# A six-layer transformer stage with its slots in a new order, an unrolled expert stage, and the softmax product on VectorE

## The reference, cut to what matters

```python
# mixture of experts: three routed linears, top 2 of 8 experts
logits = x @ router_w.T
vals, idx = top_k(logits, 2); probs = softmax(vals)
combine = einsum('tk,tke->te', probs, one_hot(idx, 8))
out = sum(combine[:, e:e+1] * (x @ expert_w[e].T) for e in range(8))

# transformer, 6 times: 16 heads of 64, windows of 32 tokens that see 64 keys
q, k, v = split(shift_tokens(x) @ Wqkv)
q = rotary(l2norm(q) * qs); k = rotary(l2norm(k) * ksc)
attn = softmax(8 * q k^T with mask)
x = (attn @ v) @ Wo + x
x = (a * gelu(gate)) @ W2 + b2 + x     # a, gate = split(norm(shift_tokens(x)) @ W1 + b1)
```

## Time and profile before

| | us |
|---|---|
| median of 3 runs | 5227.65 (5224.09 to 5231.3) |
| the profiled execution, its own time | 5220.35 |
| its span, first to last instruction | 5218.5 |
| PE busy | 4516.0 (87%) |
| DVE busy | 3483.4 (67%) |
| ACT busy | 2311.9 (44%) |
| POOL busy | 2147.3 (41%) |
| expert stage | about 110 to 1035 |
| transformer stage | about 1230 to 5218 |

### The profile page before, as it was taken

How to read it: one execution, slowest core, us unless ns; L and a number is a source line. 1 busy time by engine, 2 the same in 40 slices (tenths; PEclk the granted TensorE clock), 3 DMA queues, 4 the chain that set the end, 5 groups by cost and what they waited for, 6 DMA issues and landing times.

```text
span 5218.5 us, 147460 instructions
## 1 busy us (share of the span) xinstructions
PE 4516.0 (87%) x64229; PEld 3255.0 (62%) x64613; DVE 3483.4 (67%) x7580; ACT 2311.9 (44%) x4138; POOL 2147.3 (41%) x1332
## 2 busy tenths in 40 slices
PE   4999899885888888888888888888888888888887
PEld 3666666563666666666666666666666666666665
DVE  5434343435777777777777777777777777778884
ACT  2111111122555555555555555555555555555553
POOL 0000000003555555555555555555555555555552
PEclk7999999997999999999999989999999999999997
DMA  1000000001111111111111111111111111111110
GB/s 70 1 1 0 0 0 0 9 1 43 29 33 30 33 41 39 33 31 32 41 39 33 33 29 44 40 33 30 36 43 38 30 30 33 45 39 32 32 33 24
DMA packets 70585, 152.25 MB, mean 29 GB/s; under 512 B 14523, under 2 KB 43078, under 8 KB 69574
## 3 DMA queue, kind: packets, MB, share of 16 engines
q1 hardware_dynamic: 69958, 143.09, 9.4%
HBM read 27.69 MB, written 2.10 MB: 6 GB/s over the span
## 4 chain that ended last, share of the span: by engine, by line
PE 44%; DVE 22%; ACT 5%; issue 5%; POOL 0%; DMA 0%; SPq 0%; DVEq 0%; POOLq 0%; ACTq 0%
PE pQ L1480 8%; PE pS L1464 7%; PE pO L1524 6%; PE pC L1580 5%; PE pO L1511 4%; ACT sq L1355 4%; PE pM L1546 4%; PE pM L1535 3%; PE pT L1511 3%; DVE E L1196 3%; DVE mx L1194 2%; DVE rot L1216 2%; DVE m L1220 2%; DVE ve L1254 2%; DVE n L1231 2%
## 5 line engine op out<-in xcount | busy, mean ns | idle before, releaser
L1138 POOL TENSOR_TENSOR rot<-rot,m 128x1024 f32<-128x1024 f32 x384 | 905.1, 2357 | 602.8 <-DVE m L1220 602.8
L1130 POOL TENSOR_TENSOR rot<-rot,rn 128x1024 f32<-128x1024 f32 x384 | 731.9, 1906 | 281.1 <-DVE rn L102 281.1
L1147 POOL TENSOR_TENSOR E<-E,rc 128x512 f32<-128x512 f32 x384 | 400.5, 1043 | 943.1 <-DVE rc L1206 943.0
L1346 ACT ACTIVATE E<-E 128x512 f32<-128x512 f32 x384 | 241.7, 629 | 1091.5 <-DVE E L1196 1091.5
L1511 PE MATMUL pO<-PT,V 64*64 64x32 f32 x12288 | 482.5, 232 | 199.6 <-ACT PT L1362 199.6
L1194 DVE TENSOR_REDUCE mx<-pS 128x8 f32<-128x512 f32 x384 | 264.2, 688 | 548.6 <-PE pS L1464 548.4
L1511 PEld LDWEIGHTS pO<-PT,V 64*64 64x64 f32 x12288 | 440.9, 149 | 284.2 <-issue 284.2
L1464 PE MATMUL pS<-kT,qT 64*32 64x64 f32 x24576 | 493.1, 238 | 87.1 <-issue 57.3
L1464 PEld LDWEIGHTS pS<-kT,qT 64*32 64x32 f32 x24576 | 424.0, 120 | 172.2 <-issue 172.1
L1216 DVE TENSOR_TENSOR rot<-pQ,tabl 128x1024 f32<-128x1024 f32 x384 | 469.5, 1223 | 54.0 <-ACT sq L1355 52.0
L1511 PE MATMUL pT<-PT,V 64*64 64x32 f32 x12288 | 484.6, 233 | 0.0
(11 more groups left out here) (221 smaller groups left out, 7932.3 us busy)
## 6 DMA issues: line engine op xcount, KB each, us to landing
V<-V SPq DMA_DIRECT2D x192, 384.0 KB, 3.5
xs<-XT SPq DMA_DIRECT2D x192, 64.0 KB, 2.9
V<-V SPq DMA_DIRECT2D x96, 128.0 KB, 3.3
ys<-XT SPq DMA_DIRECT2D x192, 64.0 KB, 2.0
wq<-in_wqkv SPq DMA_DIRECT2D x6, 512.0 KB, 4.0
wk<-in_wqkv SPq DMA_DIRECT2D x6, 512.0 KB, 4.0
wv<-in_wqkv SPq DMA_DIRECT2D x6, 512.0 KB, 3.9
wo<-in_wo SPq DMA_DIRECT2D x6, 512.0 KB, 4.0
```

Of the source, the lines that this page charges most:

```text
L1130: e.tensor_tensor(r, r, rn[n % 2][:, u * HEADS:(u + 1) * HEADS].unsqueeze(2).to_broadcast([P, HEADS, HD]), ALU.mult)\
L1138: e.tensor_tensor(rot[j % RING][:, :], rot[j % RING][:, :], m2[:, :, :].rearrange("p h d -> p (h d)"), ALU.add)\
L1147: e.tensor_tensor(ev, ev, rc[:, g, :].unsqueeze(2).to_broadcast([P, NW, KEYS]), ALU.mult).then_inc(g_no.sem, 1)
```

## The change

Three things are changed.

1. In the expert stage the loop at run time is written out as straight code, and the staging copy b_xst goes, with its POOL slot and its semaphore. PE, DVE read X itself.
2. In the transformer stage the product E * rc goes from POOL (`by_sum`) to DVE, as the last instruction of `sums(B,g)` behind the reciprocal; `probs` on PE waits for DVE now.
3. The slot lists of all engines of the transformer stage are in another order. SP issues its transfers of V earlier in the pass, the weights wv at the end of the pass before, and the output later.

```diff
@@ moe_phase @@
-        xst = [sb(f"b_xst{i}", [P, L]) for i in range(2)]
...
-            run((0, 0), None)
-            run((1, 1), (0, 0))
-            with eng.Fori(0, (NSEQ - 2) // 2) as i:
-                for p in range(2):
-                    n = 2 * i + (2 + p)
-                    run((n, p), (n - 1, 1 - p))
-            run(None, (NSEQ - 1, 1))
+            for n in range(NSEQ + 1):
+                run((n, n % 2) if n < NSEQ else None, (n - 1, (n - 1) % 2) if n else None)
...
-                        e.wait_ge(gr.sem, gr.at("st", n))
...
-                            m = e.transpose(pm[0][:, t * P:(t + 1) * P], xst[p][:, t * P:(t + 1) * P], ident[:, :])
+                            m = e.transpose(pm[0][:, t * P:(t + 1) * P], X[:, n, t, :], ident[:, :])
@@ transformer_phase, gpsimd @@
-                unit_scale(R, 0)
-                root(C)
-                by_sum(B, 0)
-                rotary_add(A, 0)
-                last_root(F)
-                for k in range(1, 4):
+                for k in range(4):
                     unit_scale(R, k)
-                    by_sum(B, k)
                     rotary_add(A, k)
+                    if k == 0:
+                        root(C)
+                    if k == 1:
+                        last_root(F)
@@ vector, sums @@
                 e.reciprocal(rc[:, g, :], sm[:, g, :]).then_inc(v_r.sem, 1)
+                e.wait_ge(v_r.sem, v_r.at("rc", i))
+                ev = E[i % 2][:, :].rearrange("p (w k) -> p w k", k=KEYS)
+                e.tensor_tensor(ev, ev, rc[:, g, :].unsqueeze(2).to_broadcast([P, NW, KEYS]), ALU.mult).then_inc(v_r.sem, 1)
@@ vector, slots @@
-                statistics(C)
                 less_max(B, 0)
                 sums(B, 0)
+                rotate(A, 0)
+                statistics(C)
+                squares(A, 0)
                 normal(C)
...
@@ tensor, slots @@
                 scores(B, 0)
+                probs(Dn, 3)
                 project(A, 0)
-                probs(Dn, 3)
+                back(C)
+                attend(Dn, 3)
                 turn(R, 0)
...
@@ tensor, probs @@
-                e.wait_ge(g_no.sem, g_no.at("no", i))
+                e.wait_ge(v_r.sem, v_r.at("no", i))
```

More of the change, by code:

```diff
@@ L1084, in _ @@
                     e.dma_start(wqkv[1][:, :], I["wqkv"][A // NSEQ, :, N:2 * N]).then_inc(wqkv_l[1], 16)
-                if R and starts(R):
-                    e.wait_ge(p_v.sem, p_v.at("b", 2 * R - 1))
-                    e.dma_start(wqkv[2][:, :], I["wqkv"][R // NSEQ, :, 2 * N:3 * N]).then_inc(wqkv_l[2], 16)
                 if C and starts(C):
@@ L1102, in _ @@
                     e.dma_start(wqkv[0][:, :], I["wqkv"][(A + 1) // NSEQ, :, 0:N]).then_inc(wqkv_l[0], 16)
+                if F is not None:
+                    f = F - (NP - NSEQ)
+                    e.wait_ge(v_f.sem, v_f.at("out", f))
+                    e.dma_start(out[:, f, :, :], X[:, f, :, :]).then_inc(stored, 16)
                 if R is not None:
                     v, w = V[R % 2][:, :, 0, :], V[R % 2][:, :, 1, :]
-                    e.wait_ge(a_v.sem, a_v.at("b", 2 * R))
-                    e.dma_start(w[WIN:P, 0, :], v[0:P - WIN, 0, :]).then_inc(vs_l[R % 2], 16)
-                    e.dma_start(w[0:WIN, 1, :], v[P - WIN:P, 0, :]).then_inc(vs_l[R % 2], 16)
                     e.wait_ge(a_v.sem, a_v.at("b", 2 * R + 1))
                     e.dma_start(w[WIN:P, 1, :], v[0:P - WIN, 1, :]).then_inc(vs_l[R % 2], 16)
+                    if starts(R + 1) and R + 1 < NP:
+                        e.dma_start(wqkv[2][:, :], I["wqkv"][(R + 1) // NSEQ, :, 2 * N:3 * N]).then_inc(wqkv_l[2], 16)
             e.wait_ge(stored, 16 * NSEQ)
@@ L1305, in _ @@
                     tables(A)
-                statistics(C)
                 less_max(B, 0)
                 sums(B, 0)
+                rotate(A, 0)
+                statistics(C)
+                squares(A, 0)
                 normal(C)
-                rotate(A, 0)
-                squares(A, 0)
-                last_stats(F)
                 less_max(B, 1)
@@ L1317, in _ @@
                 squares(A, 1)
-                last_normal(F)
+                last_stats(F)
                 less_max(B, 2)
-                hidden(C, 0)
                 sums(B, 2)
@@ L1323, in _ @@
                 squares(A, 2)
+                last_normal(F)
                 less_max(B, 3)
+                hidden(C, 0)
+                sums(B, 3)
+                rotate(A, 3)
                 hidden(C, 1)
                 hidden(C, 2)
-                sums(B, 3)
-                rotate(A, 3)
-                ffn_add(C)
                 squares(A, 3)
                 roots(A)
+                ffn_add(C)
         @block.scalar
@@ L1403, in _ @@
             for A, R, B, Dn, C, F in passes():
+                probs(Dn, 3)
                 exponent(B, 0)
                 square(A, 0)
-                probs(Dn, 3)
+                heads_out(Dn, 3)
                 turned(R, 0)
-                heads_out(Dn, 3)
-                affine(C)
+                values(R, 0)
                 exponent(B, 1)
                 square(A, 1)
+                affine(C)
+                probs(B, 0)
+                turned(R, 1)
+                heads_out(B, 0)
+                probs(B, 1)
+                exponent(B, 2)
+                square(A, 2)
                 gelu(C, 0)
                 gelu(C, 1)
-                probs(B, 0)
-                turned(R, 1)
+                heads_out(B, 1)
+                turned(R, 2)
                 gelu(C, 2)
-                heads_out(B, 0)
-                exponent(B, 2)
-                square(A, 2)
-                probs(B, 1)
-                turned(R, 2)
-                heads_out(B, 1)
-                values(R, 0)
+                values(R, 1)
+                probs(B, 2)
                 exponent(B, 3)
                 square(A, 3)
-                probs(B, 2)
+                heads_out(B, 2)
                 turned(R, 3)
-                heads_out(B, 2)
-                values(R, 1)
         @block.tensor
@@ L1604, in _ @@
                 scores(B, 0)
+                probs(Dn, 3)
                 project(A, 0)
-                probs(Dn, 3)
+                back(C)
+                attend(Dn, 3)
                 turn(R, 0)
-                last(F)
-                attend(Dn, 3)
-                normed(C)
+                values(R, 0)
                 scores(B, 1)
                 project(A, 1)
+                normed(C)
+                combine(Dn)
+                probs(B, 0)
+                turn(R, 1)
                 hidden(C, 0)
-                probs(B, 0)
-                combine(Dn)
-                turn(R, 1)
+                attend(B, 0)
+                last(F)
+                scores(B, 2)
+                probs(B, 1)
+                project(A, 2)
+                attend(B, 1)
+                turn(R, 2)
                 hidden(C, 1)
-                attend(B, 0)
-                scores(B, 2)
-                project(A, 2)
+                values(R, 1)
+                scores(B, 3)
+                probs(B, 2)
+                project(A, 3)
                 hidden(C, 2)
-                probs(B, 1)
-                turn(R, 2)
-                attend(B, 1)
-                values(R, 0)
-                scores(B, 3)
-                project(A, 3)
-                contract(C)
-                probs(B, 2)
-                turn(R, 3)
-                attend(B, 2)
-                values(R, 1)
-                back(Dn)
+                attend(B, 2)
+                turn(R, 3)
+                contract(C)
 def layout(i):
```

37 lines of the change are left out of this document (10 added, 27 removed).

## The result

The changed kernel takes 5290.38 us (median of 3 runs, 5285.33 to 5291.64) against 5227.65. The ratio is 1.012, with a 95% interval of 1.0095 to 1.014: slower, 13 us under the forecast of 5303.

A forecast was written before the change was run, and what follows sets the result against it. No engine is full; a pass is a ring partly over DVE, partly over PE. 5220.35 + 155 (passes) + 5 (last layer) - 80 (expert stage) = 5300, left at 5303 us for the median; range 5195 to 5420.

The forecast's parts named there:

- The ring: Transformer pass as four segments between `less_max` on DVE and PE: 41.6 us at full clock, 3.1 over the undisturbed old order.
- Segment 3 and the product of group 1: PE from `normal(C)` to `less_max(B,2)`: 8.9 us, DVE waits 1.6 us, so the product there is hidden.
- The late Exp: Segment 1: copy `probs(B,2)` now precedes ACT's table load, so Exp starts at 2.39 instead of 1.45 us, +0.94.
- The clock: A fall to 1.2 GHz expected at the gap ahead of `contract`; half of 1.3 us taken, giving 42.2 us a pass.
- PE's new waits: PE waits about 2.5 us ahead of `contract`, 1.4 at `values(R,0)`, 1.1 at `normed`, 1.3 at `hidden(C,1)`.
- The total of the pass term: Transformer stage: +1.63 us a pass against 40.57, +155 us for 95 passes.
- The expert stage: PE's staging-copy wait goes, 53.4 us in 14 passes, plus 27 us of clock at 1.9 a pass: -80 us.
- The last layer and the ends: In the last layer F adds statistics and a norm where DVE now waits: +5 us at most.
- the removed wait decides: Rival: losing the wait at `attend(Dn,3)` makes passes 38.5 to 39.5 us, total 4990 us; chance 0.13.
- The two parts cancel: Rival: no clock falls, passes of 41.2 to 41.6 us, +60 to +98 against -80, about 5222 us; chance 0.17.
- Stalls against POOL: Rival: three products on DVE's path wait for POOL instructions, 3 us more a pass, 5590 us; chance 0.05.
- That straight code costs what the loop did: Rival: in the expert stage, fetching straight code costs as much, so that change brings nothing, 5380 us; chance 0.05.

The follow-up runs named there:

- second experiment: The whole change, but with the product (`by_sum`) back on POOL between `unit_scale` and `rotary_add`: 5119.87 us, ratio 0.979 to the kernel before.
- fifth experiment: The change, with `exponent(B,3)` and its table load ahead of the copy `probs(B,2)` on ACT: 5194.43 us, ratio 0.994 to the kernel before.
- the first: The change's expert stage alone, in front of the transformer stage of the kernel before: 5149.21 us, ratio 0.985.
- seventh experiment: The kernel before with only the expert stage's loop written out as straight code, staging copy kept: 5206.94 us, ratio 0.996.

## Why the prediction was right, point by point

The sign, the size and the mechanism came out: a pass that needs more DVE time than its removed wait was worth, less a gain in the expert stage. That the total is so near is in part luck: against the sum of the prediction the passes came out 20 us lower, the ends 10 lower and the expert stage 21 higher.

- **The ring.** Forecast at full clock 12.55 + 10.17 + 8.9 + 9.95 = 41.6; measured 12.62 + 10.17 + 9.13 + 9.83 = 41.75. Three segments are within 0.12 us. The 3.1 us more than the old order undisturbed are 3.26 at clock 1.00.
- **Segment 3 and the product of group 1.** This term was mis-sized. I held the product there for hidden behind PE; it costs 0.43 of segment 3's 9.13 us (second experiment). `attend(B,0)` waits for `attention_add` (L1221, 4064.40), which stands behind the product (4061.53) on DVE. The wait for it was counted, the product in front of it was not.
- **The late Exp.** Forecast +0.94 us, measured 1.0 when undone.
- **The clock.** I forecast 42.2 with a stretch at 1.2 GHz as long as before in half of the passes. The mean is 42.04. A short fall costs nothing, as forecast (41.75 at a mean clock of 0.96 and of 1.00). A long one costs 0.6 us instead of 1.3 and comes in 14 of the first 81 passes instead of half, but there are 5 passes of 44.0 that I had not foreseen. The two errors are of opposite sign.
- **The tables.** Missed. I looked for POOL beside the four products, found it idle, and was right there (the median of the product is 691 ns). I did not ask what else has two inputs in SBUF: `tables` now starts behind POOL's instruction, where it began ahead of it before, five times 2 us. The prediction had weighed this mechanism, but only for the four products.
- **PE's new waits.** `contract` 2.5 forecast, 2.67 in the pass shown; `hidden(C,1)` 1.3, measured 1.16; `values(R,0)` 1.4, measured 0.26; `normed` 1.1, measured 0.59. The means are 2.6, 1.2, 0.5 and 0.7. The last two lie behind a fall of the clock, which stretches PE's work and so shortens its wait. The fifth experiment fits this: 56 of its first 81 passes are at clock 1.00, and there the two waits have means of 1.1 and 1.0 us.
- **The total of the pass term.** +155 us for 95 passes; measured +134.9 for 92, which is 1.47 a pass instead of 1.63.
- **The expert stage.** -80 forecast. By itself it brings 82 us, but the changed kernel's own trace shows only 59 ahead of the first `less_max`. The wait went (53.4 us in all). The clock part failed there: I took 1.9 us a pass, and 0.8 is seen (14 passes are 65.0 us shorter, 53.4 of them the wait), since the fall at L608 stays. The kernels with the same expert code reach the first `less_max` 59 to 75 us earlier (59 in the change, 69 in the first and 75 in the second experiment), so some 15 us hang on how the falls of the clock lie: the same pass takes 50.5, 52.2 or 53.9 us. That it was the copy and not the loop that mattered is shown by the seventh experiment and by the passes with hardly a fall, 54.3 us in the loop, 54.4 in straight code, 50.5 without the copy.
- **The last layer and the ends.** +5 forecast. The books show +8.4 at the start and -13.5 at the end, for work that begins at another place of the pass; the two together are -5.

Of the rivals, "the removed wait decides" held for the old order (180 us when it alone goes, most of it clock) but not for the change, where DVE was late as the walk had it. "The two parts cancel" needed passes of 41.2 to 41.6; the undisturbed pass came near, 41.75, but the mean did not, and the trace's expert term was 59. Stalls against POOL came at `tables`, and at one of the 384 products (2.07 us). That straight code costs what the loop did is refuted.

## What to carry to other kernels

Where no engine is full, cut the pass at its handovers and walk each segment on the engine that sets it: busy shares would have called moving work from a late POOL to a DVE at 67% harmless, and it cost 170 us. Compare kernels by passes at the same clock as well as by their means: a shorter ring and a better clock are two gains, and a large part of what an edit brings can be the second. When a wait ends on an engine that has had its input for long, try first to move the one waiting instruction ahead in that engine's list; here one ACT copy moved by two places gave 3.5%, while the whole change, with the same wait removed, lost 1.2%, and its order alone, with the product left on POOL, gained 0.6% (second experiment against the first). An edit's price belongs to the order that it is measured in: measure the parts of a combined change alone and together.
